# Merging the gated FFN of a transformer layer into the steps of its attention, on one Trainium2 core

## What is computed

```python
s = softmax(mask(rope(xn @ Wq.T) @ rope(xn @ Wk.T).T / 4)) @ (xn @ Wv.T)   # 16 heads of 16, T = 1024
s = s @ Wo.T
h = fwht(xn * SU_ug) / 64                                                # Hadamard over 256
h = silu(h @ W_gate.T * ws_gate * 64) * (h @ W_up.T * ws_up * 64)        # 1024 wide
h = fwht(h * SU_dp) / 64
g = silu(h @ W_down.T * ws_down * 64)
out = X + s * g
```

## Time and profile before

| | us |
|---|---|
| median of 3 runs | 991.52 |
| lowest, highest | 987.62, 1007.11 |
| span of the profiled execution | 1012.2 |

### The profile page before, as it was taken

How to read it: one execution, slowest core, us unless ns; L and a number is a source line. 1 busy time by engine, 2 the same in 40 slices (tenths; PEclk the granted TensorE clock), 3 DMA queues, 4 the chain that set the end, 5 groups by cost and what they waited for, 6 DMA issues and landing times.

```text
span 1012.2 us, 15825 instructions
## 1 busy us (share of the span) xinstructions
PE 909.2 (90%) x5848; PEld 541.1 (53%) x5848; DVE 533.5 (53%) x868; ACT 465.3 (46%) x661; POOL 395.5 (39%) x473
## 2 busy tenths in 40 slices
PE   4599999999999998889999999999999899999824
PEld 1378787777877786444444444444444444444303
DVE  6743233424344331487776656766775575775001
ACT  2333333334333333566665555655564465565610
POOL 4584664647374644122121223421241421241424
PEclk9799999999999999699996769996997695997866
DMA  6132575242341414942446165237353402121151
GB/s 241 41 93 75 174 162 173 62 138 94 94 136 31 156 51 136 176 91 63 95 95 136 34 170 112 59 85 159 78 146 95 85 33 96 44 98 42 50 173 43
DMA packets 60458, 104.17 MB, mean 103 GB/s; under 512 B 7808, under 2 KB 22112, under 8 KB 60256
## 3 DMA queue, kind: packets, MB, share of 16 engines
q1 hardware_dynamic: 59344, 102.13, 38.2%
q10 hardware_dynamic: 1040, 1.05, 0.3%
HBM read 56.44 MB, written 46.40 MB: 102 GB/s over the span
## 4 chain that ended last, share of the span: by engine, by line
PE 44%; DVE 8%; issue 5%; POOL 1%; ACT 1%; POOLq 0%; DVEq 0%; ACTq 0%
PE ps L1036 17%; PE ps L1022 10%; PE ps L116 10%; DVE mx L1139 8%; PE ps L125 4%; PE ps L1051 3%; ACT probs L1094 1%; PE ps L1006 1%; POOL o_lo L950 1%; POOL o_n L944 0%; POOL res L957 0%; POOLq L798 0%; ACT L1094 0%; ACT o_hi L1106 0%; DVE mx_high L1145 0%
## 5 line engine op out<-in xcount | busy, mean ns | idle before, releaser
L1139 DVE TENSOR_REDUCE mx<-ps 128x1 f32<-128x512 f32 (+2 forms) x600 | 349.5, 631 | 158.4 <-PE ps L125 98.6
L1094 ACT ACTIVATE probs<-ps 128x1024 f32<-128x1024 f32 (+3 forms) x384 | 295.6, 812 | 212.5 <-PE ps L1022 210.1
L935 POOL TENSOR_SCALAR_AFFINE_SELECT probs<-probs 128x256 f32<-128x256 f32 x256 | 102.9, 406 | 366.4 <-ACT probs L1094 363.6
L116 PE MATMUL ps<-k_s,q_s 48*128 48x512 f32 (+3 forms) x768 | 217.5, 420 | 30.8 <-DVE mx L1139 28.5
L1022 PE MATMUL ps<-q_s,k_s 49*128 49x512 f32 (+3 forms) x768 | 183.0, 460 | 10.6 <-ACT probs L1094 5.5
L1036 PE MATMUL ps<-probs,v_ones 128*32 128x512 f32 (+3 forms) x1536 | 189.1, 569 | 0.1
L1022 PEld LDWEIGHTS ps<-q_s,k_s 49*128 49x128 f32 x768 | 85.3, 208 | 162.6 <-ACT probs L1094 85.2
L116 PEld LDWEIGHTS ps<-k_s,q_s 48*128 48x128 f32 x768 | 116.3, 212 | 88.6 <-DVE mx L1139 76.8
L345 POOL TENSOR_TENSOR hid_lo<-hid,hid_hi 128x512 fp32r<-128x512 f32 x64 | 82.7, 1293 | 100.8 <-ACT hid_hi L502 100.8
L561 DVE SCALAR_TENSOR_TENSOR hid<-ps,scales,silu 128x512 f32<-128x512 f32 x64 | 48.0, 749 | 131.6 <-PE ps L404 131.6
L404 PE MATMUL ps<-xh,wug_hi 128*128 128x512 f32 x256 | 103.3, 403 | 2.3 <-PEq L608 2.3
(11 more groups left out here) (94 smaller groups left out, 957.2 us busy)
## 6 DMA issues: line engine op xcount, KB each, us to landing
scr_qk<-kinds SPq DMA_DIRECT2D x96, 256.0 KB, 3.4
q_s<-scr_qk SPq DMA_DIRECT2D x32, 384.0 KB, 6.4
k_s<-scr_qk SPq DMA_DIRECT2D x32, 384.0 KB, 9.4
scr_heads<-o_raw SPq DMA_DIRECT2D x32, 256.0 KB, 4.5
x_sb<-in_x SPq DMA_DIRECT2D x8, 512.0 KB, 4.3
scr_v<-v_st SPq DMA_DIRECT2D x16, 256.0 KB, 4.1
scr_gate<-y_sb SPq DMA_DIRECT2D x8, 512.0 KB, 4.7
v_raw<-scr_v SPq DMA_DIRECT2D x16, 256.0 KB, 5.0
```

What stands on the lines that cost most here:

```text
L116: last = pe.matmul(ps[:, banks[e], n * w:(n + 1) * w], q[rows, p, i * P:(i + 1) * P], k[rows, p, part * CH:part * CH + w], start=True, sto ...
L935: pool.affine_select(out=v, in_=v, compare_op=ALU.is_ge, fill=0.0, base=0, pattern=[[0, 2], [1, P]], channel_multiplier=-1).then_inc(cut, 1)
L1094: act.activation(probs[:, s % RING, p, :, 0:w], ps[:, bank:bank + 2, 0:w], ACT.Exp, scale=SCALE).then_inc(exp_ok, 1)
L1139: dve.tensor_reduce(out, ps[:, turn_bank['tile', v, k, e], 0:n * w].rearrange('p (x k) -> p x k', x=n), axis=AX.X, op=ALU.max).then_inc(ti ...
```

## The change

The program is cut differently. `first_block` has the projection alone, with the folding of the weights spread over its chunks; `second_block` has attention and the whole FFN.

- Steps: a unit now has 10 (`STEPS` joins the narrow last key blocks into one step), and there are 171 (`NSTEP`). Unit v's 20 tiles are made two to a step in steps 10v to 10v + 9 and its scores in steps 10v + 11 to 10v + 20, so that steps 0 to 10 have no scores and 161 to 170 no tiles.
- PSUM: score products and tiles share banks 0 to 4 in a ring of pairs (`RING_PAIRS`). In the order scores 0, tile 0, scores 1, tile 1 each waits until the second and the third before it are read (`ring_before`, `wait_ring`). Banks 5 and 6 (`F_BANKS`) are for FFN jobs, bank 7 for the weighted sums.
- TensorE's step: scores 0, tile 0, the weighted sums of the step before, the step's FFN jobs (`mid_jobs`), scores 1, tile 1, and then the few jobs that found no bank (`end_jobs`).
- A FFN job is a gate or an up product (6 matmuls) or a quarter of a down product (6). There are 128 and 64; 20 of the 192 lie in steps 0 to 9, 4 in steps 161 to 164. A planner at import deals them out by a cost of 1.4; 110 steps get one in their middle, 34 get two.
- Masks: no mask matmuls. A tile on the diagonal is read by `tensor_tensor_reduce` with a triangle `tri`, one for each head, that adds it and takes the maximum; it is written back to PSUM and each is two instructions on VectorE. Tiles below the diagonal are read by one `tensor_reduce` of 1024, where their two banks are neighbours (four of five pairs), otherwise by two.
- silu(x) is x/2 (1 + tanh(x/2)): ScalarE's `Tanh`, then VectorE; ScalarE scales the up product, GpSimd multiplies and makes high and low parts.
- Queries and keys are stored in four images and put together by 10 smaller loads for each half of a unit (`load_qk`), with two buffers in place of five.

The core of the diff:

```diff
-EARLY_UNITS = (0,)
-NBUF = 5
+STEPS = [(0, (0,)), (0, (1,)), (0, (2, 3))] + [(1, (j,)) for j in range(6)] + [(1, (6, 7))]
+NS = len(STEPS)
+S_START = NS + 1
+NSTEP = S_START + NS * NU
+RING_PAIRS = ((0, 1), (2, 3), (0, 4), (1, 2), (3, 4))
+COST = {'turn': 0.45, 'gate': 1.4, 'up': 1.4, 'down': 1.4, 'piece': 1.4, 'rows': 0.0}
+EARLY_COST = 2.8
+MOST = 3
...
+    early = n
+    for k in range(n):
+        in_mid = k < early and give_bank(todo[0], 2 * g)
+        if not in_mid and not give_bank(todo[0], 2 * g + 1):
+            break
...
             for g in range(NSTEP):
-                u, s = divmod(g, NS)
-                tiles = tiles_of(g)
-                scores(u, s, 0)
-                for v, k in tiles[:1]:
-                    max_tile(v, k)
-                scores(u, s, 1)
-                for v, k in tiles[1:2]:
-                    max_tile(v, k)
...
-                if g >= LAG:
-                    weigh(*divmod(g - LAG, NS))
+                now = score_at(g)
+                tiles = tiles_at(g)
+                if now:
+                    scores(*now, 0)
+                if tiles:
+                    max_tile(*tiles[0])
+                if score_at(g - 1):
+                    weigh(*score_at(g - 1))
+                for j in mid_jobs[g]:
+                    job(j)
+                if now:
+                    scores(*now, 1)
+                if tiles:
+                    max_tile(*tiles[1])
+                for j in end_jobs[g]:
+                    job(j)
...
-                dve.tensor_reduce(out, ps[:, turn_bank['tile', v, k, e], 0:n * w].rearrange('p (x k) -> p x k', x=n),
-                                      axis=AX.X, op=ALU.max).then_inc(tile_read, 1)
+                            last = dve.tensor_tensor_reduce(part_of, part_of, sh.tri[:, CH - w:CH], 1.0, LOWEST,
+                                                            ALU.add, ALU.max, mx[:, v % 2, kind, h, i % TPC:i % TPC + 1])
...
             for g in range(NSTEP):
+                if now:
+                    exponentials(*now, 0)
+                for j in end_jobs[g - 1] if g else ():
+                    job(j)
+                if now:
+                    exponentials(*now, 1)
+                for j in mid_jobs[g]:
+                    job(j)
```

More of the change, by code:

```diff
@@ new lines @@
+ring_order = []
+for g in range(NSTEP):
+    for n in range(2):
+        if score_at(g):
+            ring_order.append(('scores', *score_at(g), n))
+        if tiles_at(g):
+            ring_order.append(('tile', *tiles_at(g)[n]))
+ring_pair = {what: RING_PAIRS[n % len(RING_PAIRS)] for n, what in enumerate(ring_order)}
+ring_before = {}
+for n, what in enumerate(ring_order):
+    before = []
+    for bank in RING_PAIRS[n % len(RING_PAIRS)]:
+        m = next((m for m in range(n - 1, -1, -1) if bank in RING_PAIRS[m % len(RING_PAIRS)]), None)
+        if m is not None and ring_order[m] not in before:
+            before.append(ring_order[m])
+    ring_before[what] = before
@@ new lines @@
+PV_BANK = 7
+F_BANKS = (5, 6)
+CHAIN = [{'load': 0, 'recip': 2, 'keep': 3, 'spread': 4, 'scale': 11, 'high': 12, 'low': 13, 'more': 14,
+          ('piece', 0): 16, ('piece', 1): 17, ('sum', 0): 17, ('sum', 1): 18, ('out', 0): 18, ('out', 1): 19},
+         {'load': 19, 'recip': 20, 'keep': 21, 'spread': 22, 'scale': 24, 'high': 25, 'low': 26, 'more': 27,
+          ('piece', 0): 28, ('piece', 1): 29, ('sum', 0): 29, ('sum', 1): 30, ('out', 0): 30, ('out', 1): 31}]
+chain_at = {}
+for b in range(B - 1):
+    for c in range(QC):
+        for what, later in CHAIN[c].items():
+            chain_at[step_of(NG * (b + 1), 2) + later, what] = QC * b + c
@@ new lines @@
+for what, later in (('load', 5), ('recip', 6), ('keep', 7), ('spread', 8)):
+    chain_at[step_of(NU - 1, later), what] = NCHUNK - 2
+at = lambda g, what: chain_at.get((g, what))
+FFN_ORDER = (NCHUNK - 1,) + tuple(range(NCHUNK - 1))
+QUARTERS = 4
+ffn_jobs = []
+for n in range(NCHUNK):
+    for ib in range(IB):
+        ffn_jobs += [('gate', n, ib), ('up', n, ib)]
+    if n + 1 < NCHUNK:
+        ffn_jobs += [('turn', n + 1, d) for d in range(DC)]
+    ffn_jobs += [('down', n, o, q) for o in range(DC) for q in range(QUARTERS)]
@@ L51 @@
+assert not todo
+for ch in range(NCHUNK - 2, NCHUNK):
+    for o in range(DC):
+        assert give_bank(('piece', ch, o), 2 * NSTEP + ch)
+job_step = {j: g for g in range(NSTEP) for j in mid_jobs[g] + end_jobs[g]}
 class Shared:
@@ L830, in attention_block @@
+        sums_in, heads_in, spread_in, more_in, inv_out = (
+            [sem(f'{name}{i}') for i in range(2)] for name in ('sums_in', 'heads_in', 'spread_in', 'more_in', 'inv_out'))
+        inv_ok, scaled, high, low = (sem('inv_ok'), sem('scaled'), sem('o_high'), sem('o_low'))
         piece_ok, gated_ok, res_ok = (sem('piece_ok'), sem('gated_ok'), sem('res_ok'))
@@ new lines, in max_tile @@
+                banks = ring_pair['tile', v, k]
+                q, keys = (q_s[v % 2], k_s[v % 2])
+                if k in (0, LOW_TILES):
+                    pe.wait_ge(sh.qk_in[v % 2][int(k > 0)], 16 * QK_LOADS * (v // 2 + 1))
+                wait_ring(('tile', v, k))
+                for n, p in enumerate(pairs):
+                    for e in range(2):
+                        rows = slice(SLOT * e, SLOT * (e + 1))
+                        last = pe.matmul(ps[:, banks[e], n * w:(n + 1) * w], q[rows, p, i * P:(i + 1) * P],
+                                         keys[rows, p, part * CH:part * CH + w], start=True, stop=True)
```

1652 lines of the change are left out of this document (841 added, 811 removed).

## The result

The changed kernel takes 1182.2 us (median of 4 runs, 1175.6 to 1192.1) against 992.9 for the kernel before in the same runs: a ratio of 1.195, 95% interval 1.189 to 1.201. It is 19% slower. The forecast was 1040 us, 5% slower, with a range from 955 to 1140.

What follows compares the result with a forecast made beforehand. It took the order of TensorE's queue, with uncovered waits in every step, as the bound: 125 + 7 + 41 + 813 + 31 + 43 = 1060 us of span, 20.7 above the median, so 1040 us, range 955 to 1140.

Steps and rivals of the forecast that it cites:

- D: Steps 11 to 160: time from scores 1's start until tile 0 can start, 2.38 us, with only two TensorE pairs inside.
- + 0.28 (tile 0) + sums + FFN jobs: Steps 11 to 160: TensorE work added behind D; with it 5.4 us a step, 813 us for 15 units.
- I take 125: Projection block: bounded by TensorE, VectorE or DMA totals, DMA 111 us behind some 12 of start; ends 110 and 150.
- Steps 0 to 10 ... 3.6, with the hand-over 41: Early steps, two jobs and two tiles each: TensorE 3.5 us, VectorE 3.6 a step, 41 us for the eleven.
- this coupling: Steps 11 to 160: VectorE's gate product queues with tile reads; charged nothing, 13 us if the cover fails.
- 1.65 + 0.28 + 0.9 and a third of a job: Steps 161 to 170: terms of one step; 31 us in all.
- The profiled span's 20.7 us above the median: Whole kernel: span sum of 1060 us lowered by this distance to 1039, say 1040.
- The masked reduce: Diagonal tile reads on VectorE: 0.79 us a head for 512 columns, 0.52 for 256; low end 0.63 for 512.
- the waits are covered: Rival, attention steps: TensorE never held at scores 0 and tile 0, 800 us; partial cover, 890 to 970 us, chance 0.15.
- The clock stays low: Rival, attention units: clock at 0.85 makes TensorE's 38.4 us 45.2, 100 us more, 1140 us; chance 0.1.

Runs made afterwards that it cites:

- jobs_end: Changed kernel with every FFN job of a step moved behind tile 1, instead of behind the weighted sums: 1003.8 us, ratio 1.020.
- spread: queue without end_pool's wait, the first unit's 20 query, key and value loads back on SyncE, five behind each of four chunks' stores: 966.1 us, ratio 0.972.
- end_first: end_pool with, in steps 0 to 9 alone, FFN jobs between the two tiles and VectorE's gate product ahead of tile 1's read: 979.1 us, ratio 0.989.
- queue: end_first with x of chunks 2 to 7 and the first unit's 20 loads issued by ScalarE instead of SyncE: 977.5 us, ratio 0.987.
- ffn_thin: Changed kernel with 896 of the 1152 wide FFN matmuls left out: 1038.1 us, single run.
- end_pool: jobs_end with the first unit's 20 loads after chunk 5's stores and GpSimd's low-part subtraction waiting for VectorE's 4-column product: 1000.4 us, ratio 1.009.

## Why the prediction was wrong

The direction was right and so was the mechanism that I gave for it: D is in every step of the plain pattern, scores 0 released by ScalarE, the middle's work unable to fill it. It measured 2.22 us where I had 2.38. That tile 0 is then released by VectorE held in 49 of 132 steps. Filling that place alone (jobs_end) makes a kernel of 1004 us. But the sum came out 143 us short, and these are its steps that failed, in the order of their size.

1. **"+ 0.28 (tile 0) + sums + FFN jobs", the terms of a step behind D**, 46 us. In the 132 steps of the plain pattern, from tile 0 to the sums are 0.48 us, not 0.28; the sums take 1.01, not 0.89; FFN 1.90, not 1.83. With D at 2.22 that is 5.60 for 5.42, some 24 us. I took the pair's price from the earlier trace rows, where scores follow a tile pair after 0.24 us. Here the sums follow it, and in 119 of the 132 steps they wait for nothing: the pair itself takes 0.42 us then. In the other 13 they wait, 8 us in all, mostly for ScalarE to copy bank 7. That 0.2 us alone is 30 us over 150 steps. The clock, 0.95 and not 1.00, is in these terms too. The other steps make up most of the rest: 17 have a Wo piece, a transpose or a FFN job behind tile 1 in the changed kernel as well and take 6.65 us each, where my sum had 5.42 for all.
2. **The first block, "I take 125"**, 42 us. I took the largest of three totals: TensorE below 100, VectorE 110, DMA 111. The totals were nearly right: 102.95 and 111.03 us, and a DMA share of 0.61, 106 us of 173.6. No single one of them bounds the block. It is a ring of fixed queues, in which VectorE's waits add to its work: 23.1 us for parts of the up and gate weights, 13.2 for x, 8.8 for GpSimd's share of the normalising. The runs account for 19 of the 42 us: SyncE's 20 loads in one place and x behind the stores (173.6 to 154.9, spread). In spread VectorE still waits 12.0 us for the weights' third and fourth part, which no run took away; how the other 23 us divide stays open. I had read the share of a bandwidth and not the queue that issues: here an issue takes 0.34 to 0.74 us of SyncE, and 20 of them are 10 us.
3. **"Steps 0 to 10 ... 3.6, with the hand-over 41"**, 26 us. I counted TensorE's and VectorE's work of a step and took the larger. The FFN job's bank comes free only behind VectorE's product, and that stood behind tile 1's read, which waits for tile 1, which stands behind the jobs. end_first took 20 us away by the order of its instructions alone, the clock's share included, and with 46.6 us it comes near the 41. For the later steps I had named this coupling and charged nothing, rightly: in steps 11 to 160 TensorE's weight loads for gate and up waited 4.2 us in all for that product.
4. **"1.65 + 0.28 + 0.9 and a third of a job", the last steps**, 20 us for ten. My terms add up to 3.3 us a step, though I wrote 31 for ten; 5.1 were measured. What I left out is GpSimd's cut behind the exponential, and the clock, 0.77 here. TensorE's matmuls waited 13.8 us in this stretch, over half of it for the cut. jobs_end shortens the stretch by 10 us, with 8.1 us of such waits and a clock of 0.93. How the 20 us divide between waits and clock was not measured. In the changed kernel's waits from 1099 us on (PEld is TensorE's weight load, which runs beside its matmuls):

```profile
PEld ps L1022 <- ACT probs L1135: 12.7, 8, 1.9
...
PE ps L1022 <- POOL probs L880: 7.3, 5, 1.7
```

5. **The profiled span's 20.7 us above the median**, carried over to another execution, 17 us.

The masked reduce was at the low end of its bounds: heads of 256 columns start 0.38 us apart for my 0.52, and of 512 columns 0.62 us apart for my 0.79 (one instruction takes 0.715 in the mean). Plain reduces of 512 columns started 0.61 us apart in the kernel before. The read-out is a second instruction, as the Trainium skill has it ("VectorE: DVE Perf Modes", "Two Vector instructions with no wait between them"); the trace agrees. It takes 0.142 us, but the next head starts at the same moment (205.78 for both above), so it adds nothing that shows in these distances. Only the last of a tile stands alone.

Of the rivals, *the waits are covered* needed a D below 1.93, and this order has 2.22; in jobs_end, where most of the wait is covered, a step takes 4.58 us, still more than this rival's 3.84. *The clock stays low* was priced at 1140 and described half a truth: 0.95 in the steps, 0.77 and 0.60 at the end, but 0.82 already in the first block, whose matmuls I had priced at full clock. Before, TensorE was busy 339 of 340 us at clock 1.00; now 103 of 174. Misses 1 to 4 all have one sign: waits at hand-overs and the lower clock were left out, and the chances treated them as if they could fall either way.

## What to carry to other kernels

Where two engines hand work to each other in a ring, filler helps only in the gap in which an engine really waits. Write down, for each product that waits, what stands between it and the product it waits for; a filler behind the waiting product lengthens the step, and one ahead of it is cheap as far as the gap goes: with one job a step took 5.38 us in the first case and 4.23 in the second. A second job cost 1.3 to 1.5 us in either place (6.87 and 5.57), about its own six matmuls. Balance the gaps before you count work: the same 192 jobs cost 178 us more or less by whether they stood before scores 1 or behind tile 1. And for a stage without one busy engine, add up one round of its ring, issue times of the DMA queue included, in place of taking the largest total.

## What was unexpected of the hardware

- A product of 128 x 4 on VectorE took 2.3 us whenever it began just behind a GpSimd subtraction of 128 x 1024 from SBUF (six of eight in the changed kernel): it ended when the subtraction did. It took 0.16 us when that was kept away, and also beside a GpSimd instruction that only writes zeros (at 19.56 us in the changed kernel). It has two operands in SBUF. VectorE's own subtraction of 128 x 1024 with two SBUF operands took 2.13 to 2.27 us in the changed kernel where it began over 1 us before the end of a GpSimd operation on SBUF, and 1.21 us in its other four cases. VectorE's rotary products, of which one operand is in PSUM, took 1.21 us beside GpSimd's work and without it. The Trainium skill ("VectorE: DVE Perf Modes", "Two Vector instructions with no wait between them") says that VectorE reads the second of two SBUF inputs through an interface shared with GpSimd; the trace agrees.
- An issue of a load cost ScalarE's queue about the same as SyncE's: 0.4 to 0.6 us for most, up to 1.2 in the timeline of queue. Twenty-one of them took 12.7 us of ScalarE there, and twenty took 10.2 us of SyncE in the changed kernel. Moving transfers to another engine moves the price along.
- In steps 11 to 160 the granted clock was lower where TensorE had more idle time: 0.99 in jobs_end (busy 649 of 687 us), 0.95 in the changed kernel (685 of 859), 0.84 in ffn_thin (557 of 735). It is no rule across kernels: the kernel before was busy 363 of 390 us at 0.85, and steps 0 to 10 had 0.83 at 50 of 67 us in the changed kernel and 0.78 at 53 of 67 in end_pool. What sets it is not shown here.
